# One VectorE pass for mask, sign and row maximum of the attention scores

## The reference, cut to what matters

```python
# token encoder, four times
sims = jnp.einsum('bqd,bkd->bqk', q, k) * scale
sims = jnp.where(causal_mask[None, :, :], jnp.float32(-1000000000.0), sims)
attn = jax.nn.softmax(sims, axis=-1)
enc = jnp.einsum('bqk,bkd->bqd', attn, enc)
...
# block attention; with 256 tokens (4 blocks) the top 8 blocks are all past blocks
qk = jnp.where(causal, qk, -INF)
p = jax.nn.softmax(qk, axis=-1)
o = jnp.einsum('bhst,bthd->bshd', p, v).reshape(B, S, H * D)
```

## Time and profile before

| | |
|---|---|
| median of 3 runs | 2302.99 us (2301.66 to 2303.2) |
| span of the profiled execution | 2301.2 us |
| TensorE busy | 2220.2 us (96%) |
| VectorE busy | 1656.8 us (72%) |
| ScalarE busy | 715.0 us (31%) |
| GpSimd busy | 381.6 us (17%) |

### The profile page before, as it was taken

The page is one execution under the profiler, slowest core; times in us unless marked ns, Lnnn a source line. Parts: engine busy times, 40 slices in busy tenths (PEclk is TensorE's granted clock), DMA queues, the critical chain, the costliest instruction groups (busy, mean ns, idle before and its releaser), DMA issues.

```text
span 2301.2 us, 31084 instructions
## 1 busy us (share of the span) xinstructions
PE 2220.2 (96%) x11962; PEld 1130.5 (49%) x11962; DVE 1656.8 (72%) x3357; ACT 715.0 (31%) x1603; POOL 381.6 (17%) x416
## 2 busy tenths in 40 slices
PE   6777899999999999999999999999999999999999
PEld 4666444444444444444445555555555554444444
DVE  7767799998998886576766665665665677588832
ACT  5667423122122112444333333333333333211111
POOL 3453100000000330622050002100400300401000
PEclk9889999999999999999999999999999999999999
DMA  6767733333323333221231112311311223100001
GB/s 188 223 185 215 244 131 106 108 133 119 126 98 119 124 126 117 60 81 53 71 94 35 35 29 53 90 29 35 101 35 35 63 65 62 60 1 1 1 1 74
DMA packets 195683, 202.73 MB, mean 88 GB/s; under 512 B 148944, under 2 KB 161872, under 8 KB 186576
## 3 DMA queue, kind: packets, MB, share of 16 engines
q1 hardware_dynamic: 195248, 199.70, 29.0%
q10 hardware_dynamic: 288, 1.05, 0.1%
HBM read 137.28 MB, written 27.26 MB: 72 GB/s over the span
## 4 chain that ended last, share of the span: by engine, by line
PE 86%; DVE 6%; issue 3%; ACT 2%; POOL 1%; DMA 1%; SPq 0%; DVEq 0%; POOLq 0%
PE ps L794 22%; PE ps L250 14%; PE ps L1415 9%; PE ps L806 7%; PE ps L1218 7%; PE ps L1231 6%; PE ps L687 5%; PE ps L1047 4%; PE ps L1064 4%; PE ps L1256 2%; PE ps L264 2%; PE ps L500 1%; PE ps L1259 1%; PE ps L262 1%; PE ps L641 1%
## 5 line engine op out<-in xcount | busy, mean ns | idle before, releaser
L794 PE MATMUL ps<-planes 128*128 128x512 f16 x1224 | 269.7, 379 | 0.0
L794 PE MATMUL ps<-planes,wa 128*128 128x512 f16 x1080 | 237.8, 379 | 2.1 <-DVE planes L1521 2.1
L250 PE MATMUL ps<-planes,wa 128*128 128x512 f16 x840 | 192.3, 379 | 3.2 <-DVE planes L1774 3.2
L794 PEld LDWEIGHTS ps<-planes 128*128 128x128 f16 x1224 | 119.8, 98 | 141.5
L834 ACT ACTIVATE work<-work 128x512 f16<-128x512 f32 x64 | 40.3, 630 | 440.1 <-DVE work L867 440.1
L250 PE MATMUL ps<-planes 128*128 128x512 f16 x768 | 175.9, 379 | 0.9 <-DVE planes L667 0.9
L794 PEld LDWEIGHTS ps<-planes,wa 128*128 128x128 f16 x1080 | 105.6, 98 | 127.5 <-issue 2.6
L311 ACT ACTIVATE ps<-ps,nmax 128x128 f32<-128x128 f32 x160 | 54.4, 340 | 307.5 <-DVE nmax L305 307.5
L621 POOL TENSOR_TENSOR rstd<-rstd,half 128x4 f32<-128x4 f32 x16 | 17.9, 1117 | 754.3 <-DVE rstd L616 754.2
L949 DVE COPY_PREDICATED work<-work 128x1024 f32<-128x1024 int16 x144 | 119.6, 830 | 21.3 <-DVE work L931 0.5
L931 DVE TENSOR_SCALAR work<-work,lutx,par 128x256 int32<-128x256 int32 x384 | 128.1, 408 | 0.0
(11 more groups left out here) (199 smaller groups left out, 4242.9 us busy)
## 6 DMA issues: line engine op xcount, KB each, us to landing
planes<-rw SPq DMA_DIRECT2D x17, 2048.0 KB, 8.5
wa<-rw SPq DMA_DIRECT2D x15, 2048.0 KB, 7.3
stg<-in_rw_w SPq DMA_DIRECT2D x32, 512.0 KB, 4.9
stg<-in_ff_w SPq DMA_DIRECT2D x16, 1024.0 KB, 5.6
rw<-wa SPq DMA_DIRECT2D x16, 1024.0 KB, 7.7
stg<-in_mo_w SPq DMA_DIRECT2D x16, 1024.0 KB, 5.6
work<-in_glu_idx SPq DMA_DIRECT2D x48, 128.0 KB, 2.1
glu_dec<-work SPq DMA_DIRECT2D x48, 128.0 KB, 1.7
```

The source lines that it names most:

```text
L250: mm = te.matmul(ps[:, bank, :], w(i, kt), x(j, kt), start=(kt == 0 and n == 0), stop=(kt == KT - 1 and n == 2))
L794: mm = te.matmul(ps[:, what, :], rw_w(q, what, i, kt, m), mix[what][j][:, kt, at:at + CH], start=(kt == 0 and z == 0), stop=(kt == KT - 1 ...
```

## The change

One VectorE operation per row block, `tensor_tensor_reduce`, adds a mask, multiplies by -1, writes the result in place and gives the minimum of the results, which is the negated row maximum. There are four such operations for a unit, two of 128x128 and two of 128x256; for the wide ones `causal` grows to 256 columns, 128 of zeros before the mask. ScalarE's exponentials take the flipped scores with scale -1. The semaphore `masked` and its wait are gone.

```diff
-        causal = sb("causal", [P, P], F32)
+        causal = sb("causal", [P, 2 * P], F32)
...
         def dve_max(dve, u):
             dve.wait_ge(scored, u + 1)
-            mask = causal.rearrange("p (b k) -> p b k", b=1).to_broadcast([P, 2, P])
-            for x in (ps[:, 2, 0:S].rearrange("p (b k) -> p b k", b=2), ps[:, 3, :].rearrange("p (b k) -> p b k", b=2)[:, :, P:S]):
-                ins = ve.tensor_tensor(x, x, mask, ALU.add)
-            ins.then_inc(masked, 1)
-            dve.wait_ge(masked, u + 1)
-            ve.tensor_reduce(nmax[:, 0:2], ps[:, 2, 0:S].rearrange("p (b k) -> p b k", b=2), AX.X, ALU.max, negate=True)
-            ve.tensor_reduce(nmax[:, 2:4], ps[:, 3, :].rearrange("p (b k) -> p b k", b=2), AX.X, ALU.max, negate=True).then_inc(row_max, 1)
+            for b in range(2):
+                x = ps[:, 2, b * P:b * P + P]
+                ve.tensor_tensor_reduce(x, x, causal[:, P:2 * P], -1.0, 3.0e38, ALU.add, ALU.min, nmax[:, b:b + 1])
+                x = ps[:, 3, b * S:b * S + S]
+                ins = ve.tensor_tensor_reduce(x, x, causal[:, :], -1.0, 3.0e38, ALU.add, ALU.min, nmax[:, 2 + b:3 + b])
+            ins.then_inc(row_max, 1)
 
         def act_exp(act, u):
             act.wait_ge(row_max, u + 1)
             for b in range(2):
                 x = ps[:, 2, b * P:b * P + P]
-                se.activation(x, x, ACT.Exp, bias=nmax[:, b:b + 1], accum_out=rsum[:, b:b + 1])
+                se.activation(x, x, ACT.Exp, bias=nmax[:, b:b + 1], scale=-1.0, accum_out=rsum[:, b:b + 1])
                 x = ps[:, 3, b * S:b * S + S]
-                last = se.activation(x, x, ACT.Exp, bias=nmax[:, 2 + b:3 + b], accum_out=rsum[:, 2 + b:3 + b])
+                last = se.activation(x, x, ACT.Exp, bias=nmax[:, 2 + b:3 + b], scale=-1.0, accum_out=rsum[:, 2 + b:3 + b])
             last.then_inc(exps, 1)
...
-                ve.tensor_copy(causal[:, :], mask32[:, 0:P])
+                ve.memset(causal[:, 0:P], 0.0)
+                ve.tensor_copy(causal[:, P:2 * P], mask32[:, 0:P])
```

More of the change, by code:

```diff
@@ L160, in build @@
             "q_ps", "k_ps", "q_hi", "k_hi", "q_split", "k_split"))
-        scored, masked, row_max, exps, inv_sum, probs = (sem(x) for x in (
-            "scored", "masked", "row_max", "exps", "inv_sum", "probs"))
+        scored, row_max, exps, inv_sum, probs = (sem(x) for x in (
+            "scored", "row_max", "exps", "inv_sum", "probs"))
         pT_ps, pT_hi, pT_split = (sem(x) for x in (
```

## The result

The changed kernel took 2294.6 us (median of 5 runs, 2293.4 to 2297.4) against 2302.7 us for the kernel before on the same chip (5 runs, 2301.7 to 2303.2): a ratio of 0.9962, with an interval of 0.9950 to 0.9975. Two more comparisons of the same two kernels gave 0.9970 (0.9959 to 0.9981) and 0.9967 (0.9954 to 0.9979). Two single executions of later series, 2620.2 us of `changed_again` and 7157.1 us of `nine_units`, are slow ones and enter no ratio. The profiled execution has a span of 2292.6 us.

A forecast was written before the change was run, and what follows sets the result against it. TensorE bounds from 256 us on; in the token encoder no engine is full and waiting counts. 2.43 + 1.03 - 0.12 = 3.3 us off 2303.0 gave 2299.7 us, range 2295.5 to 2307.5.

The forecast's parts named there:

- Occupation of VectorE, before: Old `dve_max`: its four instructions were taken to occupy VectorE for about 1.74 us per unit.
- Price of the fused form: New `dve_max`: four fused operations streaming 1.10 us plus four accumulator reads of 0.09 us, 1.46 us per unit.
- the rival of cheap reads: Accumulator reads do not hold the next instruction: 1.10 us per unit, 7.4 us gained, 2295.6 us; chance 0.20.
- The rival without overlap: Each fused operation and read ends before the next: 1.71 to 2.22 us per unit, 2302.7 to 2309.4 us; chance 0.15.
- the one at half rate: Running minimum takes two cycles per element: 2.26 us per unit, 6.9 us slower, 2309.9 us; chance 0.10.
- my own case: Main forecast, reads between 0.03 and 0.15 us: 1.22 to 1.70 us per unit, about 2296.8 to 2302.6 us; chance 0.42.
- Nine places in the token encoder: Nine of sixteen `dve_max` lie on the chain that ended last; each saves 0.27 us, 2.43 us in all.
- Rival 4 (swallowed): Token encoder gain vanishes behind another path (ScalarE's list, weight split); only the last four count: about 1 us, 2302.0 us; chance 0.13.
- Only occupation counts: Token encoder: the path stays on VectorE at most of nine places, so its occupation counts, not the moment of `row_max`.
- Four late rounds: Last four `dve_max` of the block attention shorten TensorE waits: three times 0.27 us and 0.22 us, 1.03 us.
- The rest covered: 60 of 64 block attention rounds: 3.0 us between L295 and the scores cover any change, so no gain or loss.
- Memset: Added memset of 128 columns in `setup`, in front of the first unit on the chain: some 0.12 us cost.

The follow-up runs named there:

- `changed_again`: The changed kernel run again unaltered, beside three other kernels on the same chip: 2296.3 us, 0.9970 of the kernel before.
- `nine_units`: Fused operations only in token encoder units 0, 3, 4, 6, 8, 9, 11, 13, 15, old form elsewhere: 2298.1 us, 0.9984 of the kernel before.
- `pad_behind`: The changed kernel plus 0.55 us of unused VectorE reductions behind the fourth fused operation, after `row_max`: 2299.0 us, 0.9987 of the kernel before.
- `by_bank`: The changed kernel with both narrow blocks first, `row_max` raised, then both wide ones, so ScalarE starts early: 2290.5 us, 0.9946 of the kernel before.
- `pad_three`: The changed kernel plus three waited memsets of 96 columns before the first fused operation of each `dve_max`: 2306.2 us, 1.0015 of the kernel before.
- `overlap_wait`: The kernel before with the wait for `masked` split, so the first maximum waits for the first add only: 2299.4 us, 0.9988 of the kernel before.
- `attn_only`: Fused operations in the 64 block attention units only, old form in the token encoder: 2300.8 us, 0.9993 of the kernel before.

## Why the prediction was off

**Occupation of VectorE, before: right.** 1.74 us from start to next work; the trace of before has 1.72 for unit 6.

**Price of the fused form: the term that was mis-sized.** I took 0.09 us for each accumulator read, from ScalarE. The streams are as estimated or a little longer (0.21 to 0.25 and 0.38 us, for 0.21 and 0.34), but they already hold the read, which adds at most some 0.03 us each: 1.22 us where 1.46 was forecast and 1.10 was the rival of cheap reads. The rival without overlap (1.71 to 2.22) and the one at half rate (2.26) fall with the same rows. A saving of 0.52 us instead of 0.27 nearly doubles the price of a place. 1.22 us is the lower edge of my own case, for which I had 2296.8 us.

**Nine places in the token encoder: right places, wrong sum for each.** `nine_units` confirms the set. But each was counted at full value, and the table has three at nothing and one at 0.17, where GpSimd's work fixes the end of VectorE's, and one at 1.03. Nine times 0.52 would be 4.7 us; it is 3.1, against 2.4 forecast. Rival 4 (swallowed) was true for four of the nine. It named the split of the weights (L1553), but as another path and not as a brake on VectorE's own filler. My argument against it, that VectorE goes straight on, was no argument: the work it goes on with was the one that waited.

**Only occupation counts: half right.** It does in units 0, 3 and 11 (`pad_behind` is back at the old value there). In 9, 13, 15 and in the late rounds the moment of `row_max` counts, and `by_bank` earns by that alone.

**Four late rounds: right places, size partly by luck.** For the cheap reads I had 0.64 + 0.31 + 0.51 + 0.22 = 1.7 us, capped by the recorded waits, and 1.7 was measured, against 1.03 for my 0.27. But the terms are 0.45, 0.45, 0.45 and 0.37. The second and the last exceed their waits of 0.31 and 0.22: the ends of matmuls are modelled, and in the changed kernel L262 starts at 1916.82, 0.14 us before the recorded end of L1230 (1914.21 + 2.75), so the recorded wait was no cap.

**The rest covered: right.** The rounds from 18 to 76 kept their length to 0.01 us in the traces of all kernels but `pad_three`, where they lost 0.2 us in all.

**Memset: no cost seen.** The first `dve_max` started between 21.17 and 21.83 us with it and at 21.66 and 21.08 (`overlap_wait`) without.

**What the sum left out.** With the right price my sum is 3.1 + 1.7 = 4.8 us, 2298.2 from the base of 2303.0. The result is 3.6 lower. Part of it is the base: before measured 2302.7 beside the result and 2301.0 to 2301.5 in 71 runs of the later series, and the profile that I counted from is one execution in which the token encoder lost clock in places where `attn_only`, with the same code there, did not (2.06 us). Part is the clock behind `dve_max` 9: 1.7 us, lost in all four executions with the long softmax and in one of the nine with a shorter one. I named the granted clock only as something that could make the prediction wrong and gave it no term, so this is the second step that failed; the clock of the first 256 us did move, from 0.93 to 0.95. The single steps (1.45 and 1.7 us) are shown, and at this place that they go with the longer softmax. That they get rarer elsewhere when waits of TensorE get shorter fits the late rounds but is argued and not shown, and how much of the 3.6 us each cause holds stays open.

**The range** took the cheapest rival's 2295.6 us as its end without the spread of runs or the clock around it. That this rival lies only 1.0 us from the result is luck: it has 5.8 us for the nine places, where 3.1 were measured, and that error stands in for the clock and the base.

## What to carry to other kernels

Price an instruction behind which the path goes straight on by the distance to the next work that belongs to another chain, and look at what runs beside the filler on the engine that shares its memory port: an earlier start of a filler whose end is fixed by GpSimd's work is worth nothing, and a start that falls on the other side of a GpSimd operation's is worth 1 us either way. Ask of each place separately whether occupation or the signal decides, since a signal raised in the middle (ScalarE 0.75 us earlier) brought 5.8 us on top of the 5.1 of the fused operation in one comparison. And where TensorE's clock changes level from execution to execution, compare short distances that repeat to 0.02 us, not the spans of two profiles.

## What the hardware showed that I had not expected

- A fused operation's accumulator read is recorded with 0.14 us and starts with the next fused operation; with it, 128 elements start 0.21 to 0.25 us and 256 elements 0.38 us before the next. The groups by form of the changed kernel:

```profile
L303 DVE CUSTOM_DVE_ANT_0 ps<-ps,causal 128x256 f32<-128x256 f32 x160 | 74.6, 466 | 0.0
...
L303 DVE DVE_READ_ACCUMULATOR2_ANT nmax<- 128x1 f32 x160 | 22.9, 143 | 0.0
```

- Three VectorE operations beside four of GpSimd end at one and the same moment whether they start 1.22, 1.59 or 1.73 us after `dve_max` (5.97 to 5.99 us to L1755 in the eleven executions without a pad in front), while GpSimd keeps its 5.40 us.
- The granted clock fell, or did not, after equal waits of TensorE: 2.41 and 2.48 us in the token encoder, 2.05 and 2.06 in the late rounds, 1.98 and 2.03 behind `dve_max` 9. Each fall cost 1.45 to 1.7 us.
